# Shared stage: a chunk's routing choices in three parts between residual sums, and the last expert block's scatters each behind their own tile

## What the reference computes

```
x = x + attention(layernorm(x))          # latent K and V, 16 heads of 32, causal
n = layernorm(x)
probs = softmax(n @ gate_w.T)            # 8 experts
topk_w, topk_ids = top_k(probs, 2)       # weights normalised to sum 1
routed = sum over the 2 chosen e of  w_e * (silu(n @ w_gate[e]) * (n @ w_up[e])) @ w_down[e]
shared = (silu(n @ sw_gate) * (n @ sw_up)) @ sw_down
x = x + routed + shared                  # inner width 352
```

## Time and profile before

| | |
|---|---|
| median of 3 runs (lowest, highest) | 2493.39 us (2489.29, 2495.56) |
| the profiled execution: own time / its span in the trace | 2498.08 us / 2496.3 us |
| PE busy / DVE / ACT / POOL | 2293.5 (92%) / 1517.2 (61%) / 1042.4 (42%) / 1196.7 us (48%) |
| shared stage, 1474 to 1858 us of the span | 384 us: PE busy 340.8, DVE 219.6, POOL 184.5 |
| experts, 1858 to 2496.3 us | 638.3 us: PE busy 617.2, DVE 330.2, POOL 286.9 |

### The profile page before, as it was taken

How to read it: one execution, slowest core, us unless ns; L and a number is a source line. 1 busy time by engine, 2 the same in 40 slices (tenths; PEclk the granted TensorE clock), 3 DMA queues, 4 the chain that set the end, 5 groups by cost and what they waited for, 6 DMA issues and landing times. The chain is left out here.

```text
span 2496.3 us, 32769 instructions
## 1 busy us (share of the span) xinstructions
PE 2293.5 (92%) x11973; PEld 1440.7 (58%) x11973; DVE 1517.2 (61%) x3302; ACT 1042.4 (42%) x1925; POOL 1196.7 (48%) x763
## 2 busy tenths in 40 slices
PE   6997599999999999999999968999969999999997
PEld 5775344444444444444444336777758788788786
DVE  4664687767777676777767435565545555555553
ACT  3332055555555555555555542122123333333432
POOL 0100046555675655567565674545443444544543
PEclk9999599999999999999999989999989999999999
DMA  5666611314032131423212114343245656566661
GB/s 167 252 252 224 129 35 35 85 35 98 22 71 66 41 85 29 117 60 70 67 38 64 29 40 146 102 135 119 85 153 193 198 185 200 185 197 197 186 156 34
DMA packets 171616, 286.07 MB, mean 115 GB/s; under 512 B 30137, under 2 KB 72633, under 8 KB 171456
## 3 DMA queue, kind: packets, MB, share of 16 engines
q1 hardware_dynamic: 145152, 210.45, 28.8%
q0 software_dynamic: 26304, 73.54, 9.9%
HBM read 198.61 MB, written 92.38 MB: 117 GB/s over the span
## 5 line engine op out<-in xcount | busy, mean ns | idle before, releaser
L880 ACT ACTIVATE b_pt<-b_st 128x512 f32<-128x512 f32 (+3 forms) x1280 | 612.8, 535 | 492.0 <-DVE b_st L842 206.8
L697 POOL TENSOR_TENSOR b_acc<-b_acc,b_pt 128x1024 f32<-128x1024 f32 (+1 forms) x256 | 592.8, 2346 | 215.6 <-ACT b_pt L880 215.3
L821 DVE TENSOR_REDUCE b_mpart<-b_mx 128x1 f32<-128x512 f32 x768 | 511.9, 686 | 200.6 <-PE b_mx L937 198.0
L958 PE MATMUL b_st<-b_q,b_k 97*128 97x512 f32 (+2 forms) x1280 | 497.5, 401 | 75.9 <-ACT b_pt L880 54.5
L937 PE MATMUL b_mx<-b_k,b_q 96*128 96x512 f32 (+2 forms) x1280 | 508.5, 412 | 27.0 <-DVE b_mt L829 23.0
L937 PEld LDWEIGHTS b_mx<-b_k,b_q 96*128 96x128 f32 x1280 | 248.0, 195 | 283.9 <-DVE b_mpart L821 156.4
L958 PEld LDWEIGHTS b_st<-b_q,b_k 97*128 97x128 f32 x1280 | 242.4, 191 | 281.4 <-ACT b_pt L880 240.3
L971 PE MATMUL b_ob<-b_pt,b_v 128*32 128x512 f32 (+3 forms) x2560 | 304.3, 548 | 1.1 <-ACT b_pt L880 1.1
L818 DVE CUSTOM_DVE_ANT_0 b_unread<-b_mx,b_later 128x384 bf16<-128x384 f32 (+3 forms) x512 | 244.6, 484 | 90.3 <-PE b_mx L937 90.0
L697 POOL TENSOR_TENSOR b_acc<-b_pt 128x1024 f32<-128x1024 f32 x48 | 113.4, 2378 | 300.9 <-ACT b_pt L880 300.9
L69 PE MATMUL e_fb<-e_xh,e_w_guh 128*128 128x512 f32 (+1 forms) x552 | 220.5, 400 | 1.5 <-DVE e_xl L1782 1.5
(11 more groups left out here) (223 smaller groups left out, 3516.0 us busy)
## 6 DMA issues: line engine op xcount, KB each, us to landing
b_q<-scr_qh SPq DMA_DIRECT2D x64, 256.0 KB, 4.5
b_k<-scr_kh SPq DMA_DIRECT2D x64, 256.0 KB, 4.0
sw_gu<-in_L_ffn_w_gate_dram SPq DMA_DIRECT2D x12, 704.0 KB, 4.4
sw_gu<-in_L_ffn_w_up_dram SPq DMA_DIRECT2D x12, 704.0 KB, 5.8
a_xin<-in_L_attn_x_dram POOLq DMA_DIRECT2D x8, 1024.0 KB, 5.7
scr_qh<-a_qh SPq DMA_DIRECT2D x8, 1024.0 KB, 4.9
scr_ql<-a_ql SPq DMA_DIRECT2D x8, 1024.0 KB, 7.0
scr_kh<-a_kh SPq DMA_DIRECT2D x8, 1024.0 KB, 4.4
```

The lines of the kernel that those rows point to most:

```text
L697: g.tensor_tensor(out[:, :, lo:], so_far[:, :, lo:], pt[n % NPB][:, :, lo:], ALU.add).then_inc(s_add, 1)
L821: v.tensor_reduce(part, mxb[i % NMX][:, 0:w], AX.X, ALU.max).then_inc(s_red, 1)
L880: act.activation(pt[n % NPB][:, j, lo:], stb[:, (2 * n + j) % NST, lo:], ACT.Exp, scale=SCALE).then_inc(s_exp, 1)
L958: pe.matmul(stb[:, (2 * n + j) % NST, lo:], kb[:, h, at:at + P], qb[:, h, q * CH + lo:(q + 1) * CH], start=True, stop=True).then_inc(s_st, 1)
```

## The change

Three edits, with no instruction more or less but for one that changes its engine.

1. `choose` is cut in three: `choose(c, 0)` finds the first expert, `choose(c, 1)` the second and `gap`, `count_choices(c)` the counts. For all chunks but the last they no longer run ahead of `residual(c + 1)` but inside it, behind the statistics of tiles 0, 1 and 2.
2. At the start of the stage the first chunk's multiply is made by DVE and not by POOL, as DVE's first instruction, and POOL's additions for that chunk wait until DVE has made `c_ol`.
3. In the experts each scatter waits for its own tile and not for all four of its block (in every block, as the code is written), and in the last block PE finishes tiles 0 and 1 before it begins tiles 2 and 3.

```diff
                 def normalize(c, first=False):
                     if not first:
                         g.wait_ge(s_o, c * 80)
-                    g.tensor_tensor(on[:], oin[:], rin[:], ALU.mult).then_inc(s_on, 1)
+                        g.tensor_tensor(on[:], oin[:], rin[:], ALU.mult).then_inc(s_on, 1)
                     g.wait_ge(s_x, c * 16 + 16)
                     g.wait_ge(s_on, c + 1)
+                    if first:
+                        g.wait_ge(s_ol, 1)
                     for t in range(TPC):
                         ins = g.tensor_tensor(xw[:, t], xin[:, t], wob[:], ALU.add)
...
+                def choose(c, n):
...
+                    src = others if n else lg
+                    then(v.tensor_reduce(m[n][:], src[:], AX.X, ALU.max))
+                    then(v.tensor_tensor(is_max[:], src[:], m[n][:].unsqueeze(2).to_broadcast(wide), ALU.is_equal))
+                    then(v.tensor_tensor(ranked[:], is_max[:], rank[:], ALU.mult))
+                    then(v.tensor_reduce(r[:], ranked[:], AX.X, ALU.max))
+                    then(v.tensor_tensor(oh2[:, n], ranked[:], r[:].unsqueeze(2).to_broadcast(wide), ALU.is_equal))
+                    if n == 0:
+                        then(v.scalar_tensor_tensor(out=others[:], in0=oh2[:, 0], scalar=-3e38, in1=lg[:], op0=ALU.mult, op1=ALU.add))
+                    else:
+                        if c:
+                            v.wait_ge(s_ex, c)
+                        v.tensor_tensor(gap[:], m[1][:], m[0][:], ALU.subtract).then_inc(s_gap, 1)
+
+                def count_choices(c):
+                    with nc.allow_low_precision(reason="counts of at most 32 in bf16"):
+                        then(v.tensor_tensor(both[:], oh2[:, 0], oh2[:, 1], ALU.add))
+                        for t in range(TPC - 1):
+                            then(v.tensor_tensor(sooner[c % 2][:, t + 1], sooner[c % 2][:, t], both[:, t], ALU.add))
+                        v.tensor_tensor(sooner[1 - c % 2][:, 0], sooner[c % 2][:, TPC - 1], both[:, TPC - 1], ALU.add).then_inc(s_both, 1)
+
                 def residual(c, first=False):
...
                         v.tensor_tensor(x1[:, t], ab[t % 2][:], xw[:, t], ALU.add).then_inc(s_x1, 1)
                         v.wait_ge(s_x1, c * TPC + t + 1)
                         v.bn_stats(st[:, t], x1[:, t]).then_inc(s_stat, 1)
+                        if not first and t < 2:
+                            choose(c - 1, t)
+                        if not first and t == 2:
+                            count_choices(c - 1)
...
+                v.tensor_tensor(on[:], oin[:], rin[:], ALU.mult).then_inc(s_on, 1)
                 v.wait_ge(s_wh, 1)
                 v.tensor_tensor(wol[:], wos[:], f32(woh[:]), ALU.subtract).then_inc(s_wl, 1)
                 o_low(0, first=True)
...
                         token_rows(c, first)
-                        choose(c)
                         residual(c + 1)
                         norm(c + 1)
...
                 def scatter(b):
-                    g.wait_ge(s_y, b * TPB + TPB)
                     for t in range(TPB):
+                        g.wait_ge(s_y, b * TPB + t + 1)
...
                     pe.wait_ge(s_hl, b * NF + NF - 1)
-                    for t in range(TPB):
+                    ahead_of_last = range(2) if last else range(TPB)
+                    for t in ahead_of_last:
                         down(nc, fb[t][:], wt[n], hh, hl, t, range(NF - 1))
                     pe.wait_ge(s_hl, b * NF + NF)
                     for t in range(TPB):
+                        if t not in ahead_of_last:
+                            down(nc, fb[t][:], wt[n], hh, hl, t, range(NF - 1))
                         down(nc, fb[t][:], wt[n], hh, hl, t, [NF - 1]).then_inc(s_dn, 1)
```

More of the change, by code:

```diff
@@ L1366, in o_low, with then @@
                     v.tensor_tensor(ol[:], on[:], f32(oh[:]), ALU.subtract).then_inc(s_ol, 1)
+                done = [0]
+                def then(ins):
+                    done[0] += 1
+                    ins.then_inc(s_rv, 1)
+                    v.wait_ge(s_rv, done[0])
+                def choose(c, n):
+                    if c == 0 and n == 0:
+                        v.wait_ge(s_rc, NRC)
+                    v.wait_ge(s_ltc, c * 2 + 2)
+                    wide = [P, TPC, E]
+                    src = others if n else lg
[16 more added lines that the diff above has]
+                        v.tensor_tensor(sooner[1 - c % 2][:, 0], sooner[c % 2][:, TPC - 1], both[:, TPC - 1], ALU.add).then_inc(s_both, 1)
                 def residual(c, first=False):
@@ L1432, in _ @@
                 v.reciprocal(rsum[:], sums[:]).then_inc(s_rs, 1)
[L1434 to L1458, removed]
-                    v.tensor_tensor(gap[:], m[1][:], m[0][:], ALU.subtract).then_inc(s_gap, 1)
-                    with nc.allow_low_precision(reason="counts of at most 32 in bf16"):
-                        then(v.tensor_tensor(both[:], oh2[:, 0], oh2[:, 1], ALU.add))
-                        for t in range(TPC - 1):
-                            then(v.tensor_tensor(sooner[c % 2][:, t + 1], sooner[c % 2][:, t], both[:, t], ALU.add))
-                        v.tensor_tensor(sooner[1 - c % 2][:, 0], sooner[c % 2][:, TPC - 1], both[:, TPC - 1], ALU.add).then_inc(s_both, 1)
                 def slots(c):
@@ L1497, in step @@
                         token_rows(c)
-                        choose(c)
+                        for n in range(2):
+                            choose(c, n)
+                        count_choices(c)
                         hidden(c, 0)
```

## The result

| | before | after |
|---|---|---|
| median (lowest, highest; runs) | 2495.27 us (2488.79, 2499.65; 20) | 2479.55 us (2472.38, 2491.37; 20) |
| ratio after / before | | 0.9942, 95% interval 0.9929 to 0.9955 |
| span of the profiled execution | 2496.3 us | 2485.0 us |
| shared stage, first weight cast (`c_woh`) to the experts' first transposes | 1474.07 to 1857.85 = 383.78 us | 1477.06 to 1850.36 = 373.30 us |
| from there to the span's end | 638.4 us | 634.6 us |

The median fell by 15.7 us; the interval of the ratio is 11 to 18 us. The spans differ by only 11.3, because in the profiled execution after, the stages ahead, which the change doesn't touch, ended 3.0 us later. So the traces are compared by distances from the start of the stage, not by positions in the span: 10.5 us of the gain lie in the shared stage and 3.8 behind it, 14.3 in all.

A forecast was written before the change was run, and what follows sets the result against it. PE sets the shared stage's pace, DVE and POOL its start, the tail behind PE's last matmul the experts' end. Gains 9.7 + 1.2 + 3.6 = 14.5 us take the median from 2493.4 to 2478.9 us, range 2472 to 2486.

The forecast's parts named there:

- A chunk, 1.38 us: Shared stage: DVE reads tile 0's bank before the choices, so PE runs through and tile 3's last matmul starts 1.38 us earlier.
- Seven times of it, 9.7 us: Shared stage: the 1.38 us saved in each of 7 chunks, 9.7 us in all; bounds 0 and 9.7.
- The start, 1.2 us: Stage's start: first multiply on DVE, POOL's additions held; tile 0's sum 1.2 us earlier, bounds -1.3 and 3.2.
- How the clock takes such a pause: First chunk: whether PE's clock falls when PE idles after tiles 0 and 1, costing up to 5.5 us, 2.5 if back midway.
- That case: Rival: the clock falls in the first chunk, gain 12.0 instead of 14.5 us, median 2481.4; chance 0.15.
- the 2.5 that was worked out: First chunk: us lost on the 24 matmuls of tiles 2 and 3 if the clock falls and comes back midway.
- the loss of 1.3 us: Stage's start: by the skill's clock rule the start edit loses about 1.3 us (1.2 - 2.5).
- The row from which the prediction read the fall: Profile's busy row at 1466: granted clock 0.51, said to be only some 2 us behind dense work.
- The tail, 3.6 us: Experts' last block: the fourth scatter starts at 2483.7 instead of 2487.27, 3.6 us saved; bounds 2.1 and 3.9.
- The bound of 2.1 for the waits alone: Last block: lower bound of the gain, 0.68 us a tile, were PE's new tile order worth nothing.
- Port races: Rival: POOL's multiply delays DVE's `c_hl`, 1.1 us each; all six lost 2483.3, none 2476.8; more races lost, chance 0.08.
- The slower rival's threshold: Shared stage: slower needs 1.8 us a chunk lost against before, 3.1 against plan, so choices would have to double; chance 0.02.

The follow-up runs named there:

- spare matmuls: Changed kernel plus nine matmuls whose results nothing reads, between tiles 1 and 2 of the first chunk: 2480.03 us, ratio 0.9943; two further kernels also had them.
- the tail's two kernels: Kernel before with only the scatters' waits and PE's last-block order changed: 2489.11 us, ratio 0.9975; with only the scatters' waits changed: 2493.57 us, ratio 0.9993.

## Why the prediction was right, and where it was off

The forecast was 14.5 us and a median of 2478.9; measured were 14.5 by the ratio (15.7 by the medians) and 2479.55. That the figures meet so closely is in part luck: in the pair of traces the start gave 1.0 less than forecast and one lost race fewer gave 1.2. Step by step:

- **A chunk, 1.38 us: right, 1.42.** The forecast for a chunk with no lost race was 41.8, measured 41.64 to 41.67. The layout of DVE's work came out within 0.15 us everywhere. Tile 0's part was to be done 0.05 before tile 1 was ready; it was done 0.01 after, harmless as said. The counts were to have 0.28 to spare and had 0.23. Neither `positions` nor tile 3's sum waited.
- **Seven times of it, 9.7 us: right, with a detour.** The first period shrank by only 0.2 between the two profiled executions (46.74 to 46.51). But the three other kernels whose choices were as before took 47.85 to 47.95 there: in the trace of before the clock had come back 2.5 us earlier behind the stage's start than in any of them. Against these the first period too gained 1.4. With the one lost race fewer the six other periods gained 9.8, of which 8.5 are the change's.
- **The start, 1.2 us: wrong in the step that chose.** The gain up to the first sum was 1.8, more than reckoned, since the additions and the low parts took 9.7 us in turns and not 10.1, and DVE's multiply began at once. But the step "How the clock takes such a pause" left it open and the sum took the side on which the clock stays. Of six traces with the start edit and without spare matmuls it fell in five, behind pauses of 2.27 to 3.11 us; in the sixth (all parts behind tile 3) the pause was 1.90 and it stayed. That case had been given 0.15. Its price was 1.6, not the 2.5 that was worked out, as the clock came back before tile 3 was through. Net it was 0.2 us in the place of 1.2, small enough to leave the sum right. Of the rule cited in the prediction, from the Trainium skill (TensorE: Matmul & The Clock Gate, section HAM oscillation), the traces bear out one half: waits between short bursts send PE back to the low clock. The other half, that the next burst starts cold, they don't: in four of the five PE first ran on at 1.00 for 1.2 to 1.4 us. And the loss of 1.3 us, worked out beside that rule, didn't come. The row from which the prediction read the fall, stands less far behind PE's work than it says: two short groups of matmuls ran up to 1465.3, and the clock was low from 1466.0.
- **The tail, 3.6 us: right, 3.58.** Last scatter 10.34 behind (10.3 forecast), first `e_rows` 4.03 behind (4.05), PE held by `e_hl` by about 0.2. The bound of 2.1 for the waits alone was measured as 2.0.
- **Port races: as said, a matter of chance.** Two were lost in before's trace, one after, three with the choices alone, none with the scatter waits alone, whose shared stage is that of before.
- **The slower rival's threshold: right on the side, too mild in size.** It said that the choices would have to double before the change loses. Doubled, the kernel is 0.8% slower than before. But the 3.1 us a chunk named there (the stage lost 26.7, or 3.8 for each of seven) left out that such a pause can take the clock down, and that the last chunk pays the doubled choices in full.

What stays open: why the clock, behind the same wait of 2.8 us, fell in four chunks and not in the other three; and how much of the 14.5 us of the ratio is chance. The times go with the mean granted clock of the execution: the changed kernel took 2491.4 us at 0.963, 2486.2 to 2488.3 at 0.967 and 2475.3 to 2477.1 at 0.971. The kernel before, in the 70 executions measured beside the experiments, took 2504.6 and 2505.0 at 0.963, 2494.4 to 2501.2 at 0.967 and 2486.4 to 2491.9 at 0.971. At the same mean clock the two are thus some 11 us apart. Part of the difference to 14.5 is the end of the program, which the change shortens and where the clock is low (the last 9.7 us of the span before, 6.4 after); whether the rest is chance isn't shown. The 14.3 us measured from the stage's start in the two traces leave out the stages ahead, where the clock was low for 104 us in either.

## What to carry to other kernels

Where two banks alternate, what must come in time is the instruction that empties a bank; put small work behind the first such instruction, not ahead of it, and look at what follows in PE's queue (here the counts) before putting more there: against their place between the sums, the same choices cost 0.5 us a chunk more all behind tile 0, 1.4 more ahead of all sums and 7.5 or more behind them all. A lead that is won on PE ahead of a fixed wait turns into a longer pause, and the price of a pause is the clock behind it: read the granted clock in windows of 1 us there before booking the gain. And when the work ahead of the change scatters by more than the change is worth, measure from a common landmark in the traces.

## What the runs showed of the hardware

- The clock fell not in the pause of 2.35 us but 1.3 us after PE had begun again, in the midst of dense matmuls. Behind the pauses of 2.27, 2.33 and 2.40 in three other kernels it did the same after 1.2 to 1.4; behind the longer one of 3.11, in the kernel with doubled choices, it had fallen 0.3 us before PE began. So a falling clock need not show in the pause itself.
- In the first chunk the clock came back after about 10 us in the trace of before, and after nearly 14 in those of the tail's two kernels, whose shared stage is the same: 1.1 us of difference in the time of one chunk.
- Six chunks of the changed kernel's trace showed a second meeting of DVE and POOL, for which PE didn't wait. While DVE ran `c_ol` (128 x 2048, two SBUF inputs, 1693.12 to 1695.39), POOL's indirect DMA into `scr_table`, 0.96 us in the median, lasted 3.38; the other five lasted 2.42 to 3.37.
